# Expert stage of a fused attention and mixture-of-experts kernel: second layer two tiles behind the first, rows turned four ahead, two TensorE updates a tile

## The reference, cut to what matters

```python
def reference(x, ctx, g_xattn, g_ffn, Wq, Wk, Wv, Wp, bp, gate, w0, w1, wo):
    # x, ctx: (128, 64, 128) float32: 8192 tokens of 128 numbers
    x = x + tanh(g_xattn[0]) * attention(layernorm(x), ctx, ctx)      # 16 heads of 8, rope
    z = layernorm(x)
    top2, idx = top_k(z @ gate, 2)                                    # 8 experts, two a token
    w = softmax(top2)
    # expert e of a token: (silu(z @ w0[e]) * (z @ w1[e])) @ wo[e],  w0, w1: 128x256, wo: 256x128
    return x + tanh(g_ffn[0]) * sum(w[i] * expert(idx[i], z) for i in (0, 1))
```

## Time and profile before

| | us |
|---|---|
| median of 3 timed runs | 549.89 (549.31 to 550.67) |
| span of the profiled execution | 665.6 |
| time of the profiled execution around its span | not recorded |
| TensorE busy in it | 561.5 (84%) |
| VectorE, ScalarE, GpSimd busy | 393.9, 431.8, 384.0 |

### The profile page before, as it was taken

How to read it: one execution, slowest core, us unless ns; L and a number is a source line. 1 busy time by engine, 2 the same in 40 slices (tenths; PEclk the granted TensorE clock), 3 DMA queues, 4 the chain that set the end, 5 groups by cost and what they waited for, 6 DMA issues and landing times.

```text
span 665.6 us, 21070 instructions
## 1 busy us (share of the span) xinstructions
PE 561.5 (84%) x6123; PEld 468.0 (70%) x6124; DVE 393.9 (59%) x1418; ACT 431.8 (65%) x1090; POOL 384.0 (58%) x524
## 2 busy tenths in 40 slices
PE   8998898998989899899898779787778978888960
PEld 6886676776767677677776668676677868877860
DVE  6797787777778677677778643372133323223663
ACT  4897787887787788788777735344244546556540
POOL 3347756576575666657566466575545555545651
PEclk9999999999999999999999899897899999999995
DMA  3801111111111111111112112233222222225996
GB/s 91 240 20 57 42 42 52 36 55 40 48 44 36 56 40 48 48 33 58 41 55 63 33 50 73 64 98 101 85 64 80 77 74 76 76 68 174 270 272 206
DMA packets 64242, 52.98 MB, mean 80 GB/s; under 512 B 8607, under 2 KB 60064, under 8 KB 64176
## 3 DMA queue, kind: packets, MB, share of 16 engines
q1 hardware_dynamic: 46560, 30.79, 16.5%
q0 software_dynamic: 8448, 16.93, 7.7%
q10 hardware_dynamic: 9168, 4.46, 2.3%
HBM read 29.44 MB, written 23.22 MB: 79 GB/s over the span
## 4 chain that ended last, share of the span: by engine, by line
PE 51%; another core or an unknown queue 15%; issue 10%; ACT 8%; DVE 6%; ACTq 3%; DMA 2%; DVEq 2%; POOL 1%; SPq 1%; POOLq 0%
PE psK L583 10%; PE psH L603 8%; PE psH L483 5%; PE psH L489 4%; PE psG L498 4%; PE psH L498 3%; PE psK L471 3%; ACT wcur L757 3%; PE psO L619 2%; ACTq L319 2%; ACT ys L771 2%; PE psK L619 2%; ACT hs L764 2%; PE psO L518 2%
## 5 line engine op out<-in xcount | busy, mean ns | idle before, releaser
L1251 POOL DMA_INDIRECT results<-ys,zin x136 | 136.1, 1001 | 106.5 <-ACT ys L771 68.3
L603 PE MATMUL psH<-zT,wcur 128*128 128x128 f32 (+1 forms) x760 | 139.1, 333 | 20.1 <-ACT wcur L757 15.2
L1178 POOL DMA_INDIRECT lists<-zp,dest x128 | 129.6, 1012 | 34.8 <-issue 31.1
L603 PEld LDWEIGHTS psH<-zT,wcur 128*128 128x128 f32 x760 | 112.8, 195 | 34.4 <-ACT wcur L757 20.1
L1083 DVE TENSOR_TENSOR hm<-psH,hs 128x512 f32<-128x512 f32 x68 | 47.0, 692 | 121.0 <-remote 45.7
L977 DVE TENSOR_REDUCE mx<-psH 128x8 fp32r<-128x512 f32 x128 | 82.5, 686 | 43.4 <-PE psH L483 23.6
L696 ACT ACTIVATE ex<-psH,rs 128x512 f32<-128x512 f32 x128 | 86.8, 688 | 23.9 <-PE psH L489 16.3
L583 PEld LDWEIGHTS psK<-v,pT 128*64 128x64 f32 x2048 | 69.6, 137 | 37.1 <-issue 36.3
L583 PE MATMUL psK<-v,pT 128*64 128x64 f32 x2048 | 81.1, 226 | 9.0 <-issue 8.6
L757 ACT COPY wcur<-w 128x512 f32 x95 | 56.1, 619 | 15.2 <-issue 14.2
L747 ACT COPY v<-kvr 64x64 f32<-64x64 f32 x256 | 63.7, 249 | 2.2
(11 more groups left out here) (176 smaller groups left out, 1140.5 us busy)
## 6 DMA issues: line engine op xcount, KB each, us to landing
yy<-results SPq DMA_DIRECT2D x16, 512.0 KB
zin<-lists SPq DMA_DIRECT2D x41, 130.0 KB
out_dram<-x ACTq DMA_DIRECT2D x16, 256.0 KB
xring<-in_x_dram SPq DMA_DIRECT2D x31, 128.0 KB
cring<-in_ctx_dram SPq DMA_DIRECT2D x31, 128.0 KB
zin<-lists SPq DMA_DIRECT2D x54, 65.0 KB
results<-ys,zin POOLq DMA_INDIRECT x136
w<-in_L_ffn_w_kernel_dram SPq DMA_DIRECT2D x2, 1024.0 KB, 7.1
```

Source lines behind the costliest of these rows:

```text
L603: last = pe.matmul(bank[t.buf(2)][:, k * ET + c.start:k * ET + c.stop], wcur[:, t.buf(2), h, a, k * P:(k + 1) * P], zT[:, t.buf(2), c], st ...
L1178: nc.gpsimd.indirect_dma_start(lists, bass.IndirectOffsetOnAxis(ap=dest[:, t.buf(4), j:j + 1], axis=0), zp[:, t.buf(4), j, :], None).then_ ...
L1251: nc.gpsimd.indirect_dma_start(results, bass.IndirectOffsetOnAxis(ap=zin[:, t.buf(8), h, D:D + 1].bitcast(U32), axis=0), ys[:, t.buf(8), h ...
```

## The change

`second_layer(s)` now stands behind `first_products(s+2)`, and `rows_turned(s+4)` behind it, at the end of the step. ScalarE's and VectorE's orders follow: `silu(s+2)`, `weights(s+4)`, `outputs(s)` and `products(s+2)`, `inputs(s+4)`. `wcur` and `hm` get a third buffer. TensorE updates two semaphores a tile: `ab_ps` after the whole first layer, and `zy_ps` after the transposes, which tells of the second layer ahead of them too; the last four tiles, with no transposes behind them, update it after the second layer. The second half of the first layer now waits for `h_done`, the first half for `silu_done` only. `take` waits for `y_sb` of tile t - 7, and the takes of tiles 60 to 67 stand ahead of a fetch and not behind it. All expert steps are written out (`steady=NET + 1, turns=0`). By hand: tiles 0 to 3 are turned and the first layers of tiles 0 to 2 done ahead of the second layer of tile 0.

```diff
-EXPERTS = Pipeline(NET, behind=1, ahead=2, unroll=8, steady=18, turns=2)
+EXPERTS = Pipeline(NET, behind=1, ahead=4, unroll=8, steady=NET + 1, turns=0)
...
-        wcur = sb("wcur", [P, 2, 2, 2, HID])
+        wcur = sb("wcur", [P, 3, 2, 2, HID])
-        hm = sb("hm", [P, 2, 2, ET])
+        hm = sb("hm", [P, 3, 2, ET])
...
+        def rows_are_turned(eng, t):
+            eng.wait_ge(zy_ps, t.k + 1)
+        def results_there(eng, t, back=0):
+            if t.k >= back:
+                eng.wait_ge(zy_ps, t.k - back + 5)
...
                     if t.turn is not None or t.k >= 8:
-                        wait_for(sp, y_sb, t, back=6)
+                        wait_for(sp, y_sb, t, back=7)
...
                 for k in range(CHUNKS_EARLY):
-                    fetch(k)
                     if NEARLY + 8 + k < NET:
                         take(Tile(8, None, NEARLY + 8 + k))
+                    fetch(k)
...
+                def rows_turned(t):
+                    rows_there(pe, t)
+                    wait_for(pe, ez_sb, t, back=2)
+                    for h in range(2):
+                        last = pe.transpose(psZ[t.buf(2)][:, h * P:(h + 1) * P], zin[:, t.buf(8), h, 0:D], ident[:, :])
+                    last.then_inc(zy_ps, 1)
+                def first_products(t):
+                    wait_for(pe, w_done, t)
+                    wait_for(pe, ez_sb, t)
+                    for a, (bank, free) in enumerate(((psA, silu_done), (psB, h_done))):
+                        wait_for(pe, free, t, back=2)
+                        for k in range(2):
...
+                    last.then_inc(ab_ps, 1)
+                def second_layer(t, signal):
...
+                    wait_for(pe, h_done, t)
+                    wait_for(pe, y_sb, t, back=2)
+                    if t.k == 0:
+                        pe.wait_ge(on_done, NT)
+                    if t.k == 1:
+                        for n in (x1_done, oT_sb):
+                            pe.wait_ge(n, NT)
...
+                    if signal:
+                        last.then_inc(zy_ps, 1)
...
                 def experts_step(s):
                     if static(s, NFULL):
                         pe.wait_ge(late_table, LATE_READY)
-                    rows_turned(s)
-                    first_products(s)
-                    second_layer(s)
+                    if (t := EXPERTS.at(s, 2)) and t.k > 2:
+                        first_products(t)
...
+                    if t := EXPERTS.at(s, 0):
+                        second_layer(t, signal=not EXPERTS.at(s, 4))
+                    if t := EXPERTS.at(s, 4):
+                        rows_turned(t)
...
-                rows_turned((None, -1))
+                rows_turned(Tile(8, None, 1))
                 attention_step((None, NT - 2))
-                rows_turned((None, 0))
+                rows_turned(Tile(8, None, 2))
...
-                first_products((None, 0))
+                first_products(Tile(8, None, 1))
                 attention_step((None, NT - 1))
+                rows_turned(Tile(8, None, 3))
+                first_products(Tile(8, None, 2))
                 pe.wait_ge(wo_ready, E)
                 pe.wait_ge(early_table, EARLY_READY)
-                pe.wait_ge(on_done, NT)
-                second_layer((None, 0))
-                for n in (x1_done, oT_sb):
-                    pe.wait_ge(n, NT)
-                EXPERTS.run(pe, experts_step, since=1)
+                EXPERTS.run(pe, experts_step, since=0)
...
+                def weights(t):
+                    e = [expert(act, t, h) for h in range(2 if late(t) else 1)]
+                    wait_for(act, ab_ps, t, back=3)
...
                 def experts_step(s):
-                    if static(s, NFULL - 2):
+                    if t := EXPERTS.at(s, 2):
+                        silu(t)
+                    if static(s, NFULL - 4):
                         act.wait_ge(late_table, LATE_READY)
-                    weights(s)
-                    silu(s)
-                    outputs(s)
+                    if t := EXPERTS.at(s, 4):
+                        weights(t)
+                    if t := EXPERTS.at(s, 0):
+                        outputs(t)
...
+                def products(t):
+                    wait_for(dve, ab_ps, t)
+                    wait_for(dve, silu_done, t)
+                    results_there(dve, t, back=3)
...
                 attention_step((None, NT - 2))
-                inputs((None, 0))
-                products((None, -1))
+                inputs(Tile(8, None, 2))
+                products(Tile(8, None, 0))
                 attention_step((None, NT - 1))
+                products(Tile(8, None, 1))
+                inputs(Tile(8, None, 3))
                 attention_step((None, NT))
-                products((None, 0))
+                experts_step((None, 0))
```

More of the change, by code:

```diff
@@ L78, in run @@
             body((None, t))
-        with eng.Fori(0, self.turns) as turn:
-            for u in range(self.unroll):
-                body((turn, u))
+        if self.turns:
+            with eng.Fori(0, self.turns) as turn:
+                for u in range(self.unroll):
+                    body((turn, u))
         for t in range(self.steady + self.unroll * self.turns, (self.last if until is None else until) + 1):
@@ new lines, in first_products @@
+                def first_products(t):
[4 more added lines that the diff above has]
+                        for k in range(2):
+                            for h, c in enumerate((slice(0, P), slice(P, ET)) if late(t) else (slice(0, ET),)):
+                                last = pe.matmul(bank[t.buf(2)][:, k * ET + c.start:k * ET + c.stop],
+                                                 wcur[:, t.buf(3), h, a, k * P:(k + 1) * P],
+                                                 zT[:, t.buf(2), c], start=True, stop=True)
+                    last.then_inc(ab_ps, 1)
@@ L989, in attention_step @@
                     if static(s, NT - 2):
-                        inputs((None, -1))
+                        inputs(Tile(8, None, 1))
                     if (t := ATT_DVE.at(s, 4)) and t.buf(2):
```

128 lines of the change are left out of this document (47 added, 81 removed).

## The result

The changed kernel takes 556.4 us (555.89 to 557.26, 4 runs), before takes 549.94 beside it: the ratio is 1.0117, 95% interval 1.0094 to 1.0139, so 1.2% slower. The forecast was 551.5 with a range of 545.3 to 554.5; the time lies 1.9 above that range.

A forecast was written before the change was run, and what follows sets the result against it. GpSimd's scatters, not TensorE's updates, were taken to hold the middle of the expert stage. TensorE's +0.1 and the last scatters' +1.5 sum to +1.6 us on the median 549.89, giving 551.5; range 545.3 to 554.5.

The forecast's parts named there:

- Late updates belong to the recorded execution: Whole kernel: TensorE's late updates explain the 115.7 us by which the recorded span exceeds the timed median.
- 6 us of waits, 5.0 of them for rows at GpSimd's worst point; after 6.9: Expert stage: TensorE waits for tile 28's rows, held by GpSimd's scatters, 5.0 us before the change and 6.9 after.
- the floor: Expert stage: shortest step of a tile when nothing waits, 2.84 us, or 2.90 for a late tile.
- Its 6.1: TensorE's waits in the expert stage before: 5.0 for rows, 0.34 before tile 1, about 0.8 at the very end.
- 191.9: Floor in us from second layer 0 to second layer 67: 40 steps of 2.84 and 27 of 2.90.
- Rows four ahead cost one step: From second layer t - 8 to tile t's transposes: 4 steps (11.4 us) instead of 5 (14.2); wait at tile 28 grows 1.9.
- Fewer updates, order in the step, take's back=7, take ahead of fetch cost nothing: Expert steps: these parts cost no time, being hidden by the two steps of lead or by other waits.
- The end: Kernel's end: TensorE ends at the same time, +0.1 us; the last scatters, on which the end hangs, cost 1.5.
- The last second layers: End of expert stage: before, second layer 67 waits about 0.8 us for h; after, layers 65 to 67 follow at 0.89.
- The fourth rival: Tiles' last stretch: DMA engines nearly full, rows land late, deciding from a load of 6 us on; 556, chance 0.12.
- Bunching: Kernel's end: last results come together, so GpSimd ends 6.9 us after TensorE instead of 4.4; cost 2.5.
- The discount of one us for a backlog in both: Kernel's end: with a GpSimd backlog in both kernels the cost of 2.5 shrinks towards 0.5; 1.5 was taken.

The follow-up runs named there:

- third look: The kernel before, unchanged, profiled once more for a record with TensorE's full clock between the last attention tiles; span 549.0 us.
- second look: The kernel before, unchanged, profiled again to see whether TensorE's late updates come back; span 547.0 us.
- a_four: The kernel after with four TensorE updates a tile again, the two added ones waited for by nobody; 556.23 us.
- a_fetch_first: The kernel after with SyncE's fetch ahead of the take again, as before the change; 556.02 us.
- a_noload: The kernel after, TensorE taking expert 0 for second layers of tiles 65 to 67 instead of reading their experts from the table; 556.47 us in one run.
- a_lists_later: The kernel after with GpSimd's eight scatters of lists in steps 18 to 32 instead of 6 to 20; 555.03 us.

## Why the prediction was wrong, point by point

The prediction's terms laid over the same stretches, against the third look at before:

| stretch | before | after | difference | predicted |
|---|---|---|---|---|
| start of second layer 0 | 330.14 | 331.48 | +1.34 | +1.34 (1.98 - 0.64) |
| tile 0 to 40 | 118.36 | 120.53 | +2.17 | +1.56 (0.34 + 5.0 to 6.9) |
| tile 40 to 56 | 46.37 | 46.37 | 0 | 0 |
| tile 56 to 67 | 33.29 | 34.32 | +1.03 | -2.81 (30.69 to 27.88) |
| end of tile 67 to last scatter's end | 4.49 | 6.50 | +2.01 | +1.5 |
| from there to the end of the span | 15.19 | 13.84 | -1.35 | 0 |
| sum | | | +5.2 | +1.6 |

Against the second look (547.0) the sum is +7.2; the medians say +6.5. The -1.35 of the last row is one execution's (the second look has 13.83 there). The length of the last second layer, 1.15 us in both, is left out.

- **Late updates belong to the recorded execution.** Right: spans of 547.0 and 549.0 without them. That after's record would show them too (610 to 640) was wrong; they came in one record of three of before and not in after's.
- **6 us of waits, 5.0 of them for rows at GpSimd's worst point; after 6.9.** Right in mechanism and nearly in size: 4.8 above the floor in before and 6.9 in after over tiles 0 to 40, of which the buffers are 3.2 and 6.0. The 5.0 for before were too many by 1.8, and the agreement that the prediction took as support is in part luck. Its 6.1 counts 0.8 for the last step on top of 191.9, but by its own terms that step is 0.89 + 0.8 = 1.69, so 1.21 below the 2.90 that the 191.9 holds for it: its terms give 4.1. From tile 0 to 67 the third look has 6.1 above 191.9 and the second 3.1. Moving the list scatters moved the waits; 12 buffers removed them; what the start gained was lost again. In after the waits came at tiles 12 to 29 and not only for rows of 20 to 30.
- **Rows four ahead cost one step.** Right: 2.8 measured as 6.0 - 3.2, and 1.72 given back for 1.7. But it was priced in the middle only, and the last stretch paid for it too.
- **Fewer updates, order in the step, take's back=7, take ahead of fetch cost nothing.** Right for updates (`a_four`) and take and fetch (`a_fetch_first`); back=7 was not run by itself. Not right for ScalarE's order: in late tiles results leave 1.46 us later than in before, since two copies of weights and two reads of the table now stand ahead of them. The prediction kept 0.95 us from TensorE to GpSimd; from the floor's end of a second layer (0.89 behind its start) to its first scatter are 1.64 us in before and 3.10 in after for tile 56.
- **The end.** This is the step that failed. The prediction let TensorE run from tile 28 to the end without a wait for rows ("It ends at the same time, +0.1"), and let GpSimd wait last for tile 65, with "0.95 of way and three tiles of 2.56 to go". In after TensorE waits for rows in the last stretch too, and GpSimd waits last for tile 63. Up to there the loss is complete: tile 63's second layer starts at 521.98 against 516.85, 5.13 later (3.51 of it up to tile 56), and its first scatter 4.74 us behind that against 2.54, 2.20 more. ScalarE's order is the larger part of that; with the fetches gone 0.8 of it is absent. From there to the last scatter's end after is 0.8 quicker. In all 6.5, where the prediction had 1.6; with 12 buffers all of it is gone.
- **The last second layers.** The prediction put 0.8 us ahead of before's last second layer down to h, and let second layers 65 to 67 of after follow each other at 0.89. In after it is the two table reads ahead of every late second layer: 1.50 and 1.92 us from one second layer to the next with the fetches gone, 2.00 and 2.38 in after. In before h of tile 67 is there at 527.11 and its second layer starts at 528.16, so it isn't h; that it is the reads there too is not shown. The first layer of 1.79 covers them in nearly every other step; in before only tile 67 lacks this cover, in after tiles 66 and 67 do. On TensorE, 2.60 of the 2.81 to be won were lost there (4.38 - 1.78), 1.64 of it with the fetches gone (3.42 - 1.78). But it is not what made the kernel slower: without the reads (`a_noload`) the last scatter ends no earlier, and GpSimd's last wait lies at tile 63 in both.
- **The last stretch is DMA's.** The fourth rival, at 0.12, was nearest in time (556) and right in kind: with the fetches gone, or with 12 buffers, nothing waits for rows there. Its size was luck, since it asked for loads of more than 6 us. The chain of waits in after shows one case from end to end:

```profile
506.43 6.29 DMA results<-ys,zin
...
512.98 0.33 SPq L399
...
514.36 0.48 SPq L389
...
515.12 0.56 SPq L389
...
516.75 3.12 DMA zin<-lists
...
519.92 0.44 PE psX L602 x2
```

A landing of 6.29 us (2.08 in the earlier trace rows) holds SyncE, and the load itself takes 3.12; behind the take that waited stand a fetch and the next take, whose own table reads take 0.48 and 0.56; the next rows land at 519.87, and TensorE has waited. After has 3.84 us above the floor from tile 56 to 65: 3.3 in the three steps whose transposes wait for rows, 0.54 ahead of tile 65. Before has 2.1 to tile 66, none of it for rows (0.5 by the profile for `wcur`). With the fetches gone there is 0.1 up to tile 64. I priced the load of rows there and not the landing, nor SyncE's queue, nor the reads.
- **Bunching.** 6.50 us from TensorE's end to the last scatter's, 6.9 predicted at its upper bound, 4.49 (4.4 predicted) in before. Right in number, but by luck: GpSimd was still at tile 64 when tile 65's results came (its first scatter starts 2.14 us behind them, against 0.82 where it is idle), and TensorE's end was late by the reads; without them the distance is 9.4 us (`a_noload`). The discount of one us for a backlog in both was not right.

Laid over the third look, 3.8 us more than predicted lie in tiles 56 to 67, 0.6 in the middle and 0.5 in the last scatters: 4.9, as much as 551.5 lacks of 556.4. This leaves out the -1.35 of the last row.

What stays open: why the last stretch of `a_lists_later` took 2.9 us more, and what in the DMA traffic makes a table read slow; long and short reads stand beside the same share.

## What to carry to other kernels

Moving an operation ahead in the order shortens the way of its input by as many steps: count the buffers against the whole way (copy out, scatter, landing, queue, load) at the point where the slowest engine is furthest behind, and add buffers before lead. Look at what a sequencer does between two operations; register reads that a long operation covers come bare where the order puts two short ones together, as at the end of a pipeline. Before you price such an idle time, find the last wait of the engine that ends last: what lies behind it costs nothing. When two stages are swapped on one engine, go through the order of every engine that answers it.

## What the runs showed of the hardware

The Trainium skill ("Runtime: NRT & Kernel Launch", Instruction fetch mechanics) has some 200 ns for a register and calls loads round trips; it speaks there of registers that the runtime loads. For the table here, in SBUF, the trace shows more.
- An update of TensorE costs nothing that shows at these shapes: `a_four`, with two more a tile, stayed at the time of after (556.23 against 556.4). The Trainium skill ("TensorE: Matmul & The Clock Gate", The cost: per-tile semaphore tail) has 26.3 ns for each increment, an estimate of 3.6 us for two more on 68 tiles. Its figure is for increments of small matmuls packed side by side in the array, so no run here tests it where it was taken; carried over to this kernel it did not hold.
- TensorE's granted clock can fall for a few us between the last attention tiles. The window from 323 to 326 us in before, second look, and then third look:

```profile
323.00:326.00 3.00, 3.00 (x7) 2.41 (x8) 0.18 (x3) 0.68 (x2) 1.09 (x1) 0.50 0.26 70
```

```profile
323.00:326.00 3.00, 3.00 (x44) 2.38 (x42) 0.69 (x3) 0.00 (x0) 1.09 (x1) 1.00 0.44 119
```

0.50 is the lower level of 1.2 GHz. In the second look idle times of TensorE of 0.33, 0.84 and 0.61 us came before it, in the third look 0.33 and 0.61. One first layer took 3.48 us instead of 1.97, and tile 0 started 2.26 us later. By tile 28 that was down to 0.32 us, since GpSimd held the middle.
